# Moving the shared FFN of the first two batches from the routing block into the last two bodies of the attention block

## The reference

```
h = h + attention(layernorm(h))
x = layernorm(h)                                    # 16 x 375 tokens, 128 channels
probs = softmax(x @ gate_w)                         # 16 experts
scores, tok_idx = top_k(probs.T, cap)               # each expert picks 375 of the 6000 tokens
y = (gelu(x[tok_idx] @ w1 + b1) @ w2 + b2) * scores
routed = zeros.at[tok_idx].add(y)
shared = gelu(x @ sw1 + sb1) @ sw2 + sb2            # every token, hidden size 512
out = h + routed + shared
```

## Time and profile before

| what | us |
|---|---|
| median of 3 runs | 1319.2 |
| lowest and highest run | 1317.66 and 1322.45 |
| profiled execution, device time | 1321.67 |
| profiled execution, span of the instructions | 1319.9 |
| PE busy in the span | 1187.9 (90%) |
| DVE busy | 892.8 (68%) |
| ACT busy | 731.5 (55%) |
| POOL busy | 408.1 (31%) |

### The profile page before, as it was taken

The page is one execution under the profiler, slowest core; times in us unless marked ns, Lnnn a source line. Parts: engine busy times, 40 slices in busy tenths (PEclk is TensorE's granted clock), DMA queues, the critical chain, the costliest instruction groups (busy, mean ns, idle before and its releaser), DMA issues. The chain is left out here.

```text
span 1319.9 us, 23142 instructions
## 1 busy us (share of the span) xinstructions
PE 1187.9 (90%) x7812; PEld 995.4 (75%) x7812; DVE 892.8 (68%) x2614; ACT 731.5 (55%) x1845; POOL 408.1 (31%) x379
## 2 busy tenths in 40 slices
PE   6999999999988999999999999999995998766673
PEld 6999999999976777777777777777763767545562
DVE  5656566656659888888998888888865886221210
ACT  2444534344448787888877878888872342222220
POOL 5000001202003443232344432321111002688885
PEclk9999999999989999999999999999997998878877
DMA  5100000000000000000000000000001100455542
GB/s 140 33 13 23 14 13 24 13 24 13 1 25 13 13 14 26 26 27 26 26 19 16 20 26 26 25 14 13 11 19 50 30 18 26 95 91 90 91 81 29
DMA packets 91799, 42.92 MB, mean 33 GB/s; under 512 B 31066, under 2 KB 88007, under 8 KB 91687
## 3 DMA queue, kind: packets, MB, share of 16 engines
q1 hardware_dynamic: 67207, 33.49, 9.4%
q0 software_dynamic: 23808, 6.69, 4.0%
q10 hardware_dynamic: 672, 1.31, 0.3%
HBM read 28.22 MB, written 9.65 MB: 29 GB/s over the span
## 5 line engine op out<-in xcount | busy, mean ns | idle before, releaser
L487 PE MATMUL bank<-h1hl,W2hl 128*128 128x376 f32 x1536 | 279.5, 338 | 2.7 <-DVE h1hl L643 2.7
L487 PEld LDWEIGHTS bank<-h1hl,W2hl 128*128 128x128 f32 x1536 | 265.8, 190 | 7.4 <-issue 4.3
L1051 ACT ACTIVATE P<-P,nmax 125x375 f32<-125x375 f32 (+2 forms) x384 | 189.0, 507 | 2.1 <-DVE nmax L1180 2.0
L587 ACT ACTIVATE h<-bank,b2c 128x375 f32<-128x375 f32 x128 | 73.6, 575 | 209.8 <-PE bank L487 209.8
L226 POOL TENSOR_SCALAR cellmax<-grid,csb 125x375 f32<-125x375 f32 x96 | 122.9, 1292 | 212.5 <-DVE csb L219 134.7
L1180 DVE CUSTOM_DVE_ANT_0 P<-bank,nbias 125x375 f32<-125x375 f32 (+2 forms) x384 | 138.8, 409 | 1.4 <-PE bank L898 1.4
L1061 ACT COPY PT<-bank 128x500 f32<-128x500 f32 (+1 forms) x256 | 128.5, 556 | 7.6 <-PE bank L911 6.9
L898 PE MATMUL bank<-QK 64*125 64x375 f32 (+2 forms) x768 | 116.9, 408 | 9.8 <-DVE nmax L1180 9.7
L911 PE MATMUL bank<-ident,P 125*128 125x125 f32 x768 | 113.5, 275 | 0.6 <-ACT P L1051 0.4
L1646 ACT ACTIVATE hE<-bank,EB 128x375 f32<-128x375 f32 x64 | 36.8, 574 | 134.5 <-PE bank L1595 131.8
L1069 ACT ACTIVATE tap<-bank,qkd 128x375 f32<-128x375 f32 x128 | 68.5, 570 | 69.7 <-PE bank L947 69.5
(11 more groups left out here) (209 smaller groups left out, 2332.0 us busy)
## 6 DMA issues: line engine op xcount, KB each, us to landing
X<-in_x_dram SPq DMA_DIRECT2D x31, 375.0 KB
EW<-in_L_ffn_w_dram SPq DMA_DIRECT2D x32, 256.0 KB
token_table<-row SPq DMA_DIRECT2D x16, 210.9 KB
tTall<-tT SPq DMA_DIRECT2D x16, 187.5 KB, 2.5
out_dram<-oS SPq DMA_DIRECT2D x16, 187.5 KB
tTall<-in_L_tok_W_dram ACTq DMA_DIRECT2D x1, 1024.0 KB, 8.8
EB<-in_L_ffn_b_dram SPq DMA_DIRECT2D x16, 62.5 KB
tok<-token_table,ids POOLq DMA_INDIRECT x48
```

Of the source, the lines that this page charges most:

```text
L487: last = nc.tensor.matmul(bank[4 + m % 2][:, :NE], W2hl[:, a, k, m * 128:(m + 1) * 128], h1hl[:, p, b, k], start=(k == 0 and n == 0), stop ...
L587: nc.scalar.activation(h2[:, p, m], bank[4 + m % 2][:, :N], ACT.Gelu, bias=b2c[:, m:m + 1]).then_inc(s_g2, 1)
L1051: nc.scalar.activation(P[:, 2 * r + q, SEG[i]:SEG[i] + w], P[:, 2 * r + q, SEG[i]:SEG[i] + w], ACT.Exp, bias=nmax[:, 2 * r + q, i:i + 1], ...
```

## The change

Two batches (HB = 2) of the shared FFN leave block three. Their eight units are written into bodies 16 and 17 of block two, in order of PE: hidden units 0 and 1 of batch 0 in steps 0 and 2 of body 16; both hidden units of batch 1 and the first half of batch 0's output in step 3, behind the output projection; the second half in step 6; the first half of batch 1's output in step 7, the second in step 2 of body 17. They use banks that are idle there, and `QK` holds the hidden layer. ACT gets the eight gelus in steps 1 and 3, behind them a tiny exp (`warm2`) so that the table of exp is back before the softmax. DVE adds the output to `Hall` in steps 1 and 3 of body 17, and SP stores `Hall` of these batches straight to the output.

```diff
+                        if (b, h) == (B, 0):
+                            shared_h(0, 0)
...
+                        if (b, h) == (B, 2):
+                            shared_h(0, 1)
...
+                        if (b, h) == (B, 3):
+                            shared_h(1, 0)
+                            shared_h(1, 1)
+                            shared_y(0, 0)
...
+                        if (b, h) == (B, 6):
+                            shared_y(0, 1)
...
+                        if (b, h) == (B, 7):
+                            shared_y(1, 0)
+                        if (b, h) == (B + 1, 2):
+                            shared_y(1, 1)
...
+                def gelu_shared(j):
+                    for m in range(DC):
+                        act.wait_ge(s_sh, 4 * j + m + 1)
+                        if (j, m) == (0, 0):
+                            act.wait_ge(s_sp, 8 * B)
+                        nc.scalar.activation(QK[:, j, m], (G0, G1)[m % 2][:, :N], ACT.Gelu_apprx_tanh,
+                                             bias=sb1c[:, m:m + 1]).then_inc(s_shr, 1)
...
+                        if (b, h) == (B, 1):
+                            gelu_shared(0)
+                        if (b, h) == (B, 3):
+                            gelu_shared(1)
+                            nc.scalar.activation(warm2[:], zsb[:, 0:4], ACT.Exp)
...
+                for j in range(HB):
+                    sp.wait_ge(s_sr, j + 1)
+                    sp.dma_start(out[j].rearrange("(t p) c -> p t c", p=PT_), Hall[:, j]).then_inc(s_first, 16)
...
-            UNITS = 4 * (B + 1)
+            NB = B - HB
+            UNITS = 4 * (NB + 1)
```

More of the change, by code:

```diff
@@ L125, in build @@
         HEAD = 4
+        HB = 2
         zsb = sbm("zsb", [128, N])
@@ L159, in build @@
         s_zs = sem("s_z_stored")
+        s_first = sem("s_first_outputs_stored")
         PASSES = ((0, 0), (0, 1), (1, 0))
@@ L781, in build @@
             pTs = sb_("pTs", [E, N])
+            warm2 = sb_("warm2", [128, 4])
             bS, bT, bO = (bank[0], bank[1]), (bank[2], bank[3]), bank[4]
@@ L819, in build @@
             s_ps = sem("s_probsT_stored")
+            s_sh = sem("s_first_shared_h_in_psum")
+            s_shr = sem("s_first_shared_h_ready")
+            s_sy = sem("s_first_shared_y_in_psum")
+            s_sr = sem("s_first_shared_sum_ready")
             s_on = [sem(f"s_waits_passed{n}") for n in range(2)]
@@ L975, in transpose_tokens, with shared_h, shared_y @@
                     last.then_inc(done, 1)
+                def shared_h(j, q):
+                    if (j, q) == (0, 0):
+                        pe.wait_ge(s_v, 4 * B)
+                        pe.wait_ge(s_vt, 4 * B)
+                        pe.wait_ge(s_tts, 16 * HB)
+                    for m in (2 * q, 2 * q + 1):
+                        wait(pe, s_shr, 4 * j + m - 1)
+                        nc.tensor.matmul((G0, G1)[m % 2][:, :N], SW1[:, m * 128:(m + 1) * 128],
+                                         tTall[:, j * N:(j + 1) * N], start=True, stop=True).then_inc(s_sh, 1)
+                def shared_y(j, q):
+                    if q == 0:
+                        pe.wait_ge(s_shr, 4 * j + 4)
+                        pe.wait_ge(s_s, 24 * B)
+                    for i in range(6 * q, 6 * (q + 1)):
+                        t, k = i // DC, i % DC
+                        last = nc.tensor.matmul(bS[j][:PT_, t * C:(t + 1) * C], QK[:, j, k, t * PT_:(t + 1) * PT_],
+                                                SW2[:, k], start=(k == 0), stop=(k == DC - 1))
+                    if q == 1:
+                        last.then_inc(s_sy, 1)
                 def body(b, u):
@@ L1245, in body @@
                                                     ALU.mult).then_inc(s_lf, 1)
+                        if (b, h) in ((B + 1, 1), (B + 1, 3)):
+                            j = h // 2
+                            dve.wait_ge(s_sy, j + 1)
+                            dve.wait_ge(s_hb, j + 1)
+                            nc.vector.tensor_tensor(Hall[:, j], Hall[:, j], bS[j][:PT_, :NT * C].rearrange(
+                                "p (t c) -> p t c", c=C), ALU.add).then_inc(s_sr, 1)
                         if h == 1 and ahead(b + 1):
@@ L1323, in build @@
             EARLY = STEP_SUMS[-1]
-            RS = B - EARLY
+            RS = NB - EARLY
             hS = sb_("hS", [128, 2, DC, N])
@@ L1422, in _ @@
                     load_expert(sp, u, u)
-                for b in range(B):
+                for b in range(NB):
                     sp.wait_ge(s_yr, b + 1)
-                    sp.dma_start(out[b].rearrange("(t p) c -> p t c", p=PT_), oS[:, b % RS]
+                    sp.dma_start(out[HB + b].rearrange("(t p) c -> p t c", p=PT_), oS[:, b % RS]
                                  ).then_inc(s_out[b % RS], 16)
@@ L1468, in _ @@
                     gather(e, e)
-                for b in range(B - RS, B):
+                pool.wait_ge(s_first, 16 * HB)
+                for b in range(NB - RS, NB):
                     pool.wait_ge(s_out[b % RS], 16 * (b // RS + 1))
@@ L1487, in shared @@
                     turn, q = n // 4, n % 4
-                    if q < 2 and turn < B:
+                    if q < 2 and turn < NB:
                         b = turn
@@ L1493, in shared @@
                             nc.tensor.matmul(SH_B[m % 2][:, :N], SW1[:, m * 128:(m + 1) * 128],
-                                             tTall[:, b * N:(b + 1) * N], start=True, stop=True).then_inc(s_h, 1)
+                                             tTall[:, (HB + b) * N:(HB + b + 1) * N], start=True, stop=True).then_inc(s_h, 1)
                     if q >= 2 and turn > 0:
@@ L1611, in _ @@
                 pe.wait_ge(s_idx, 1)
-                pe.wait_ge(s_yc, B - EARLY)
+                pe.wait_ge(s_yc, NB - EARLY)
                 turns(pe, turn)
@@ L1632, in copy_shared @@
                                    ).then_inc(s_yc, 1)
-                for b in range(B + 1):
-                    if b < B:
+                for b in range(NB + 1):
+                    if b < NB:
                         gelu_shared(b)
@@ L1677, in decide @@
                             nc.vector.tensor_tensor(oS[:, b % RS], shared_bank(b)[:PT_, :NT * C].rearrange(
-                                "p (t c) -> p t c", c=C), Hall[:, b], ALU.add).then_inc(s_yr, 1)
+                                "p (t c) -> p t c", c=C), Hall[:, HB + b], ALU.add).then_inc(s_yr, 1)
                     nc.vector.tensor_tensor(thr[:], thr[:], grow[:], ALU.bitwise_or).then_inc(s_thr, 1)
@@ L1803, in _ @@
                     take_ids(e, e)
-                for b in range(EARLY, B):
+                for b in range(EARLY, NB):
                     dve.wait_ge(s_yc, b - EARLY + 1)
-                    nc.vector.tensor_tensor(oS[:, b % RS], oS[:, b % RS], Hall[:, b], ALU.add).then_inc(s_yr, 1)
+                    nc.vector.tensor_tensor(oS[:, b % RS], oS[:, b % RS], Hall[:, HB + b], ALU.add).then_inc(s_yr, 1)
                 take_tokens(0, 0)
```

## The result

The changed kernel took 1324.88 us (median of 20 runs) against 1320.39 us for the kernel before (20 runs). The ratio is 1.0025 with a 95% interval from 1.0017 to 1.0034, so +3.3 us, between +2.2 and +4.5: within 0.5%, and slower beyond the interval. One run of 3981.66 us is left out of the ratio.

What follows compares the result with a forecast made beforehand. No engine is full at block two's end, a one-engine-at-a-time chain; DVE paces the selection, and PE looks like the bound behind `idx`. Terms +2.4, +1.5 and -0.6 sum to +3.3 us: 1322.5 us, range 1315.5 to 1327.5.

Steps and rivals of the forecast that it cites:

- The end of block two: Last batch's chain: units ahead of its links delay it, the upper clock returns 1.4 us; +2.4 us, from +0.5 to +4.5.
- The table switch: Rival at ACT's first gelu in block two: a switch costs 2.7 us, gelus start 1.4 us later; 1323.9 us, chance 0.03.
- The second collect: Selection in block three: PE idles 3.4 us ahead of it and the clock falls; +1.5 us, from -0.7 to +4.3.
- Behind idx: Before expert 0: a wait for the gather's DMA replaces PE's queue, the lower clock takes much back; -0.6 us.
- The sum: Whole kernel: 2.4 + 1.5 - 0.6 = +3.3 us, giving 1322.5 us from the median.
- The first term: The end of block two: moved units delay the last batch's chain; +2.4 us.
- the covers hold and the clock stays up: Rival for block two, `collect` and behind `idx`: terms +0.5, 0 and -3.1, sum -2.6 us, 1316.6 us; chance 0.16.
- A longer chain in block two: Rival in block two: overrun in step 3 and a late second load; +4.5 with term at +2.9, 1326 us, chance 0.05.
- PE was the whole bound behind `idx`: Rival before expert 0: first scatter right after POOL's gathers, -6.9 us, block two costs nothing; 1312.3 us, chance 0.05.
- A clock low through the whole `collect`: Rival in block three: `collect` +4.3 us, expert 0's matmuls slow too; +6.7 to +8.2 in all, chance 0.16.

Runs made afterwards that it cites:

- the copies: Changed kernel with plain copies in place of the eight gelus in block two and without the two table loads; ratio 1.0021 to the kernel before.
- the first trace: First of three profiled executions of the unaltered changed kernel; their spans were 1321.3, 1321.1 and 1322.2 us.
- the added matmuls: Changed kernel plus 11 matmuls that nobody reads behind the last unit, while expert 0's tokens are under way; ratio 1.0015 to the kernel before.
- the filled stretch: Changed kernel with the last batch's two output units moved from behind `idx` to ahead of the second `collect`; ratio 1.0033 to the kernel before.
- the kernel with all three edits: Changed kernel with late hidden units in block two, last output ahead of the second `collect`, and 15 unread matmuls; ratio 1.0013 to the kernel before.
- the one-batch kernel: Changed kernel with one batch moved instead of two, its units only where PE idles; ratio 1.0000 to the kernel before, 0.9986 with six unread matmuls.

## Why the prediction was right, point by point

**The end of block two:** +2.4 forecast, +2.08 measured, and shown by putting the units elsewhere (24.98 us). The first unit cost 0.76 us instead of 1.0, the second 1.78 instead of 1.9. The wait for load and gelus in it was sized about right: by the prediction's working the `attend` ends at 989.1 and the unit at 990.9, 1.8 us for 1.4 us of matmuls, so a wait of 0.4, and 0.42 was measured. Only the expectation for the copies had taken 1.3 us for it; the unit's own length is the larger part. The units in step 3 fitted with 0.37 us to spare. The clock stayed up as forecast: token transposes 0.54 us, logits 0.72, last transposes 0.48. The unit in step 6 cost 0.59 us instead of 0.9: the logits were 2.78 us late where the projection was 2.54, although the transposes between them took 0.35 us less. The last unit wasn't quite free: from `probsT`'s issue to block three it took 3.34 us (1004.09 to 1007.43) instead of 3.02, 0.32 us that the forecast had at nothing. Together 2.54 - 1.37 (clock) + 0.59 + 0.32 = 2.08.

**The table switch:** the page "ScalarE: Activation LUTs" of the Trainium skill, What ACT_TABLE_LOAD costs, would have made this term an estimated +3.8. Load and gelu stand without a gap, so the measured row decides, and here a switch costs the load alone.

**The second collect:** +1.5 forecast, +0.38 in the first trace, -0.95 in the second, +0.38 in the third. Both sizes in this term were off the same way: the loss of the `collect` itself was 1.53 us where 2.2 was taken, and the small matmuls to `idx` ran at the upper clock and gave back 1.15 us where 0.7 was taken. And the clock doesn't fall in every execution: of the eight traces with the emptied stretch seven have a `collect` of 5.82 to 5.95 us and one has 4.29. The mechanism is supported by filling the stretch: 4.29 us in each of the six traces that had work there.

**Behind idx:** -0.6 forecast, -0.34, -0.45 and -0.26 measured. PE idled for 7.5 to 7.9 us and not for about 6. The tokens came at 11.8 us where 11.1 was read from the queue's bytes, so the transposes moved by 1.8 us and not by 2.5; the hidden matmuls lost 1.70 us where 2.1 was taken. The point of the forecast, that a wait for a DMA takes the place of PE's queue and the clock takes most of the rest, is shown by the added matmuls (22.00 us).

**The sum:** the stages of the first trace give +2.0 us where +3.3 was forecast (the second +1.4, the third +2.2), the runs +3.3 (2.2 to 4.5). So the agreement of the total is better than that of the terms, and that the runs gave just the forecast +3.3 is luck. Of the 19 runs without that of 3981.66 us, ten lie above 1324.7 us and nine at 1323.04 or below, and none of the three traces is from the upper group. Where its 3 to 4 us are lost is open. The first term is an unlikely candidate: it was 27.08 to 27.11 us in all six traces with these units and gelus in these places, one of them from an execution of 1326.73 us (the filled stretch). The faster matmuls of block one, seen above, could be behind the fastest runs, but that isn't shown either.

**The rivals.** That the covers hold and the clock stays up is out in two of three traces for the `collect` and in all for expert 0, and block two cost 2.08 us, not 0.5. A longer chain in block two (+4.5) wasn't seen: the units in step 3 didn't overrun. That PE was the whole bound behind `idx` is out: even with the clock kept up the first scatter gained 2.2 us, not 6.9. A clock low through the whole `collect` was never seen: the longest took 5.95 us, and twice 4.29 is 8.6.

## What to carry to other kernels

Work that moves into another stage is free only in the idle stretches of its chain, and two units of 1.4 us in the wrong one of two neighbouring places cost 2.1 us here; look at what ends the wait ahead of the place and behind it. Taking work out of an engine's queue is worth no more than the time until the next thing it waits for (here a gather that landed 11.8 us behind `idx`), and on TensorE the idle time left behind can lower the clock and take most of that back. Before moving filler away, ask whether it was also what kept the clock up. And where a change is worth 2 us in 1320, compare its stages: stretches that it doesn't touch moved by 1 to 3 us between executions.

## What the runs showed of the hardware that I had not expected

- The clock didn't fall the same way each time. With 3.48 us without work ahead of it the `collect` took 5.82, 4.29 and 5.83 us in three executions of one kernel. After 2.19 us without work, three transposes and another 0.73 us it did fall in the kernel with all three edits (hidden matmuls 5.34 us).
- The tokens of expert 0 landed 11.8 to 12.1 us behind `idx` in most kernels, but 13.4 to 13.8 us in three of them. Between `idx` and the landing the stores' queue had moved 0.83 MB in the changed kernel and 0.96 to 0.98 MB in those three, at about the same rate. In both kinds the gathers' own queue had moved 0.22 MB, the three gathers' bytes, by 10.5 to 11 us behind `idx`, so a queue's bytes, from which the prediction read 11.1 us, don't tell when the wait ends. Two of the three had the last output ahead of the `collect`, and there POOL's first gather took 4.18 us instead of 3.71. Whether the stores delay the gather or only fill a longer wait wasn't tried.
- Matmuls whose result nobody reads were worth 1.8 us between `idx` and the first scatter (22.00 us instead of 23.82), and with six of them the one-batch kernel's ratio was 0.9986 instead of 1.0000.
